# A four-stage transformer block: first distances before the second turn, squares and subtractions on GpSimd, lane loads from ScalarE's queue, preparation loads behind them

## The reference

```python
x = x + tanh(g_xattn[0]) * dtw_align(ctx, layernorm(x))     # stage 1
x = x + tanh(g_ffn[0])   * moe_64_experts_top8(layernorm(x), ...)   # stage 2
x = x + tanh(g_xattn[1]) * attention(layernorm(x), ctx, ctx, Wq..bo)  # stage 3
x = x + tanh(g_ffn[1])   * moe_8_experts_top2(layernorm(x), ...)    # stage 4
```

```python
D = sqrt(max(aa + bb - 2 * ctx @ xn.T, 0))          # 77 x 512 distances, per batch
R[i, j] = D[i, j] + min(R[i-1, j], R[i, j-1], R[i-1, j-1])
path = backtrack(R) from (76, 511) to (0, 0)
aligned[j] = sum of ctx[i] over the path's cells (i, j)
```

## Time and profile before

| what | value |
|---|---|
| median of 3 runs | 759.21 us (757.62 to 759.25) |
| the profiled execution's own time | 759.99 us |
| its span, first to last instruction | 758.3 us |
| PE / DVE / ACT / POOL busy | 656.2 / 570.3 / 397.4 / 349.5 us |
| mean granted TensorE clock | 0.903 |

### The profile page before, as it was taken

How to read it: one execution, slowest core, us unless ns; L and a number is a source line. 1 busy time by engine, 2 the same in 40 slices (tenths; PEclk the granted TensorE clock), 3 DMA queues, 4 the chain that set the end, 5 groups by cost and what they waited for, 6 DMA issues and landing times.

```text
span 758.3 us, 13278 instructions
## 1 busy us (share of the span) xinstructions
PE 656.2 (87%) x3528; PEld 502.7 (66%) x3528; DVE 570.3 (75%) x1608; ACT 397.4 (52%) x707; POOL 349.5 (46%) x326
## 2 busy tenths in 40 slices
PE   5329523889999999999999779988989999999997
PEld 2116313667888888888888546655768888888885
DVE  6579895857777777777777784889867777777775
ACT  4624220555655655565556544544456555655654
POOL 4000130565666666666666560000356666666664
PEclk9855555699999999999999968998799999999999
DMA  6565543067776776677677100000166656665761
GB/s 155 76 86 169 166 131 62 7 147 151 161 145 139 159 154 141 146 157 154 135 154 158 28 2 2 2 2 13 38 122 153 151 133 160 156 144 138 159 153 56
DMA packets 85148, 86.50 MB, mean 114 GB/s; under 512 B 41109, under 2 KB 65294, under 8 KB 82166
## 3 DMA queue, kind: packets, MB, share of 16 engines
q1 hardware_dynamic: 77340, 79.80, 49.4%
q10 hardware_dynamic: 7769, 6.25, 3.1%
HBM read 76.84 MB, written 9.17 MB: 113 GB/s over the span
## 4 chain that ended last, share of the span: by engine, by line
PE 71%; DVE 12%; DMA 5%; issue 4%; SPq 4%; ACT 2%; POOL 2%; ACTq 1%; DVEq 0%; POOLq 0%
PE bank L1203 7%; PE bank L1204 7%; PE bank_quad L1359 7%; PE bank L1205 7%; PE bank_pair L1203 7%; PE bank_quad L1356 7%; PE bank_pair L1204 7%; PE bank_pair L1205 7%; PE bank_quad L1357 7%; DMA scr_d<-arena 3%; PE bank_pair L1252 2%; PE bank L1295 2%; DVE arena L1670 1%; PE bank_pair L1175 1%; DVE rden L1799 1%
## 5 line engine op out<-in xcount | busy, mean ns | idle before, releaser
L803 POOL TENSOR_TENSOR act_lo<-arena,act_hi 128x512 fp32r<-128x512 f32 x232 | 300.3, 1294 | 191.2 <-ACT act_hi L1003 147.7
L1017 ACT ACTIVATE arena<-bank 128x512 f32<-128x512 f32 x232 | 138.8, 598 | 183.3 <-PE bank L1205 183.3
L1903 DVE TENSOR_TENSOR bank_pair<-arena,bank_pair 128x512 f32<-128x512 f32 x220 | 152.4, 693 | 99.9 <-ACT arena L1017 70.6
L1911 DVE TENSOR_TENSOR arena<-bank_pair,arena 128x512 f32<-128x512 f32 x220 | 152.1, 691 | 17.8 <-DMA arena<-scr_mask 5.7
L1003 ACT ACTIVATE act_hi<-arena 128x512 fp32r<-128x512 f32 x232 | 144.5, 623 | 14.4 <-DVE arena L1901 7.5
L1359 PE MATMUL bank_quad<-act_lo,w_hi 128*128 128x512 f32 x232 | 93.0, 401 | 4.0 <-POOL act_lo L803 4.0
L1203 PE MATMUL bank_pair<-xn_hi,w_hi 128*128 128x512 f32 x232 | 92.8, 400 | 3.5 <-DVE arena L1911 1.8
L1203 PE MATMUL bank<-xn_hi,w_hi 128*128 128x512 f32 x232 | 93.1, 401 | 0.0
L1204 PE MATMUL bank<-xn_hi,w_lo 128*128 128x512 f32 x232 | 93.1, 401 | 0.0
L1356 PE MATMUL bank_quad<-act_hi,w_hi 128*128 128x512 f32 x232 | 93.0, 401 | 0.0
L1204 PE MATMUL bank_pair<-xn_hi,w_lo 128*128 128x512 f32 x232 | 92.1, 397 | 0.0
(11 more groups left out here) (252 smaller groups left out, 981.1 us busy)
## 6 DMA issues: line engine op xcount, KB each, us to landing
arena<-scr_mask SPq DMA_DIRECT2D x94, 512.0 KB, 6.6
scr_w<-prep_out ACTq DMA_DIRECT2D x25, 192.0 KB, 2.4
w_raw<-scr_w SPq DMA_DIRECT2D x25, 192.0 KB, 6.3
w_raw<-in_L_ffn_expert_gate_k SPq DMA_DIRECT2D x32, 64.0 KB, 5.9
w_raw<-in_L_ffn_expert_up_k SPq DMA_DIRECT2D x32, 64.0 KB, 5.6
w_raw<-in_L_ffn_expert_down_k SPq DMA_DIRECT2D x64, 32.0 KB, 5.3
prep_in<-in_L_ffn_wg SPq DMA_DIRECT2D x21, 64.0 KB, 2.0
prep_in<-in_L_ffn_wu SPq DMA_DIRECT2D x21, 64.0 KB, 2.4
```

Of the source, the lines that this page charges most:

```text
L803: nc.gpsimd.tensor_tensor(act_lo[:, k % 2, :], act_a[:, k % 2, :], act_hi[:, k % 2, :].bitcast(F32), ALU.subtract).then_inc(FF[f]["alo"], 1)
L1017: nc.scalar.activation(act_s[:, k % 2, :], ps[4 + k % 2][:], ACT.Silu).then_inc(FF[f]["silu"], 1)
L1903: nc.vector.tensor_tensor(ps[6 + i][:], act_s[:, i, :], ps[6 + i][:], ALU.mult).then_inc(FF[f]["t"], 1)
L1911: nc.vector.tensor_tensor(act_a[:, i, :], ps[6 + i][:], mask[:, j, 512 * k:512 * (k + 1)], ALU.mult).then_inc(FF[f]["act"], 1)
```

## The change

It does the following.

1. The order of the front: ACT takes the first square root before it writes the zeros, which it writes in two parts (`blank`); PE does `distances(0)` before `turn(0, 1)`, then the tables; ACT's order is written out in `norm0`.
2. POOL makes the squares of batches 2 and 3 (`square`) and the subtraction of batches 0 to 2 (`POOL_SUBS`), in place of ACT and DVE.
3. `x` of batches 2 and 3 is loaded only when the keys have landed. `ctx_sb` is cleared in two parts.
4. ACT's queue loads the attention weights, all first lanes but one, and stores one of the first rows; SP's queue has all later rows and lanes.
5. SP loads 3 groups of the preparation ahead of the rows, in place of 4, and issues the first expert weights, the routers, the output bias and the ones only behind group 5.
6. PE's meeting sums stand behind groups 8 to 10 in place of 7 to 10; ACT's `split_first(0)` stands ahead of group 7.

```diff
-    PATH_AT, PREP = 22, 4
-    MEET_PARTS, VALUE_AT = {7: range(0, 4), 8: range(4, 8), 9: range(8, 12), 10: range(12, CH)}, 16
+    PATH_AT, PREP, PREP_FIRST, RAW_AT, SPLIT_GROUP = 22, 4, 3, 5, 7
+    BLANK, POOL_SUBS, POOL_SQUARES = 30, 3, 2
+    MEET_PARTS, VALUE_AT = {8: range(0, 5), 9: range(5, 9), 10: range(9, CH)}, 16
...
+        def first_lanes(engine, d, b):
+            engine.wait_ge(s_dst[b], 32)
+            load_lanes(engine, d, b, 0, FIRST_ROWS, s_dld)
+
+        def later_rows(engine):
+            for d in range(2):
+                for b in range(B):
+                    store_dist(engine, d, b, FIRST_ROWS, DIST_ROWS, s_dst2)
+
+        def later_lanes(engine):
             for b in range(B):
                 engine.wait_ge(s_dst[b], 32)
...
+            for d in range(2):
+                engine.wait_ge(s_dst2, 16 * 2 * B)
+                for b in range(B):
+                    load_lanes(engine, d, b, FIRST_ROWS, SLOTS, s_dld2)
...
             for b in range(B):
+                if b == 2:
+                    sp.wait_ge(s_ctx, 16 * len(CTX_PARTS))
                 sp.dma_start(x_res[:, TPB * b:TPB * (b + 1), :], x_t[b]).then_inc(s_x[b], 16)
...
-            raw0(1, 1)
-            for g in range(PREP):
+            for g in range(PREP_FIRST):
                 load_prep(sp, g, *prep_span(g))
-            sp.wait_ge(s_zero, 16 * -(-LSLOT // SLOTS))
+            sp.wait_ge(s_zero, 16 * -(-LSLOT // BLANK))
             for b in range(B):
                 sp.wait_ge(s_dist, b + 1)
-                for d in range(2):
+                for d in range(2 if b + 1 < B else 1):
                     store_dist(sp, d, b, 0, FIRST_ROWS, s_dst[b])
-                if b >= 1:
-                    sp.wait_ge(s_dst[b - 1], 32)
-                    for d in range(2):
-                        load_lanes(sp, d, b - 1, 0, FIRST_ROWS, s_dld)
-            sp.wait_ge(s_dst[B - 1], 32)
-            for d in range(2):
-                load_lanes(sp, d, B - 1, 0, FIRST_ROWS, s_dld)
-            later_rows(sp, 0)
-            later_lanes(sp, 0)
-            for g in range(PREP, GROUPS[1]):
+            sp.wait_ge(s_blank, 2)
+            first_lanes(sp, 0, B - 1)
+            later_rows(sp)
+            later_lanes(sp)
+            for g in range(PREP_FIRST, GROUPS[1]):
                 load_prep(sp, g, *prep_span(g))
+                if g == RAW_AT:
+                    shared0()
+                    raw0(1, 1)
+                    sp.dma_start(router[0][:], r0_w).then_inc(s_rw[0], 16)
+                    sp.dma_start(bo_all[:], bo.partition_broadcast(P)).then_inc(s_gbo, 16)
+                    sp.dma_start(router1_rows[:], r1_w).then_inc(s_rw[1], 16)
+                    sp.dma_start(scr_one.rearrange("(p c) -> p c", c=P), ones[0:TOK // P, :]).then_inc(s_one, 16)
...
+            for b in range(B):
+                normalise(0, b)
+                if b - 1 >= B - POOL_SQUARES:
+                    square(b - 1)
+            square(B - 1)
+            for b in range(POOL_SUBS):
+                pool.wait_ge(s_root, b + 1)
+                nc.gpsimd.tensor_tensor(d2[0:KROWS, b, 0:S], d2[0:KROWS, b, 0:S], droot2[0:KROWS, b, :], ALU.subtract).then_inc(s_fpool, 1)
...
+            def norm0():
+                root(0, 0)
+                blank(0, BLANK)
+                context()
+                root(0, 1)
+                high(0, 0)
+                for m, w in enumerate((Wq, Wk, Wv, Wo)):
+                    act.dma_start(w4[:, m, :], w).then_inc(s_aw, 16)
+                root(0, 2)
+                blank(BLANK, SLOTS)
+                lane_tables()
+                high(0, 1)
+                root(0, 3)
+                high(0, 2)
+                act.wait_ge(s_lc, 1)
+                dist_root(0)
+                high(0, 3)
+                for b in range(1, B):
+                    dist_root(b)
...
+            for d in range(2):
+                first_lanes(act, d, 0)
...
+            act.wait_ge(s_dist, B)
+            store_dist(act, 1, B - 1, 0, FIRST_ROWS, s_dst[B - 1])
+            for d in range(2):
+                first_lanes(act, d, 2)
+            act.wait_ge(s_gate, 32)
+            nc.scalar.activation(tgate[:], gates[:], ACT.Tanh).then_inc(s_tg, 1)
+            first_lanes(act, 1, B - 1)
             nc.scalar.activation(ctxT4[:], ctxT[:].unsqueeze(2).broadcast_to([P, B, RHEADS, KEYS]), ACT.Copy).then_inc(s_c4, 1)
-            later_rows(act, 1)
...
-            norm(0, distances)
+            turn(0, 0)
+            distances(0)
+            tables()
+            turn(0, 1)
+            turn(0, 2)
+            distances(1)
+            turn(0, 3)
+            distances(2)
+            distances(3)
...
-                inv = done(nc.vector.tensor_tensor(d2[rows, b, 0:S], d2[rows, b, 0:S], droot2[rows, b, :], ALU.subtract))
+                if b < POOL_SUBS:
+                    dve.wait_ge(s_fpool, POOL_SQUARES + b + 1)
+                else:
+                    inv = done(nc.vector.tensor_tensor(d2[rows, b, 0:S], d2[rows, b, 0:S], droot2[rows, b, :], ALU.subtract))
```

More of the change, by code:

```diff
@@ L392, in program @@
         s_dst = [sem(f"dist_stored{b}") for b in range(B)]
-        s_dst2 = [sem(f"dist_later_stored{d}") for d in range(2)]
+        s_dst2 = sem("dist_later_stored")
         s_dld = sem("dist_lanes")
@@ L544, in _ @@
             sp.dma_start(gates[:, 2:4], g_ffn.partition_broadcast(P)).then_inc(s_gate, 16)
-            sp.dma_start(router[0][:], r0_w).then_inc(s_rw[0], 16)
-            for m, w in enumerate((Wq, Wk, Wv, Wo)):
-                sp.dma_start(w4[:, m, :], w).then_inc(s_aw, 16)
+            sp.wait_ge(s_blank, 1)
+            for first in range(0, LSLOT, BLANK):
+                n = min(BLANK, LSLOT - first)
+                sp.dma_start(scr_d[:, :, first:first + n].rearrange("b c s w -> (b c) (s w)"),
+                             dl[0:B * CH, 0:n].rearrange("p s w -> p (s w)")).then_inc(s_zero, 16)
             for m, v in enumerate((bq, bk)):
@@ L550, in _, with shared0 @@
             sp.dma_start(bv_row[:], bv.rearrange("(o p) -> o p", o=1)).then_inc(s_aw, 16)
[L551 to L564, removed]
+            def shared0():
+                sp.wait_ge(s_pool, 2)
+                sp.dma_start(w_raw[:, 0, 0:I0], sg0).then_inc(FF_RAW[0][0], 16)
+                sp.dma_start(w_raw[:, 0, UP:UP + I0], su0).then_inc(FF_RAW[0][0], 16)
+                for k in range(2):
+                    sp.dma_start(w_raw[k * I0 // 2:(k + 1) * I0 // 2, 0, DOWN:DOWN + P],
+                                 sd0[k * I0 // 2:(k + 1) * I0 // 2]).then_inc(FF_RAW[0][0], 16)
             def raw0(g, j):
@@ L877, in query, with blank @@
                                      bias=bias2[:, 0:1]).then_inc(s_qhi, 1)
+            def blank(first, last):
+                nc.scalar.activation(dl[:, first:last], ones[:, 0:CW].unsqueeze(1).broadcast_to([P, last - first, CW]),
+                                     ACT.Copy, scale=0.0).then_inc(s_blank, 1)
+            def norm0():
[17 more added lines that the diff above has]
+                    dist_root(b)
             def norm(k):
@@ L881, in norm @@
                     root(k, b)
-                    if k == 0 and b == 0:
-                        context()
-                    if b >= 1 and not (k == 0 and b == B - 1):
+                    if b >= 1:
                         high(k, b - 1)
-                    if k == 0 and b == 1:
-                        lane_tables()
                     if k == 2 and b >= 2:
                         query(b - 2)
-                if k == 0:
-                    act.wait_ge(s_lc, 1)
-                    dist_root(0)
-                    high(0, B - 2)
-                    dist_root(1)
-                if k in (0, 2):
+                if k == 2:
                     high(k, B - 1)
-                if k == 2:
                     query(B - 2)
                     query(B - 1)
-            act.wait_ge(s_cz, 1)
-            for first, keys in CTX_PARTS:
+            for n, (first, keys) in enumerate(CTX_PARTS):
+                if n == 2:
+                    act.wait_ge(s_cz, 2)
                 act.dma_start(ctx_sb[first:first + keys.stop - keys.start], ctx_1024[:, keys].rearrange("b k d -> k b d")).then_inc(s_ctx, 16)
@@ L905, in _ @@
             nc.scalar.activation(root_one[:], ones[:, 0:1], ACT.Sqrt)
-            nc.scalar.activation(dl, ones[:, 0:CW].unsqueeze(1).broadcast_to([P, SLOTS, CW]), ACT.Copy, scale=0.0).then_inc(s_blank, 1)
-            norm(0)
-            for b in range(2, B):
-                dist_root(b)
-            act.wait_ge(s_gate, 32)
-            nc.scalar.activation(tgate[:], gates[:], ACT.Tanh).then_inc(s_tg, 1)
-            act.wait_ge(s_aw, 16 * 8)
+            norm0()
+            act.wait_ge(s_blank, 2)
+            for d in range(2):
+                first_lanes(act, d, 0)
+            act.wait_ge(s_aw, 16 * 7)
             nc.scalar.activation(wq_hi[:], w4[:, 0, :], ACT.Copy)
@@ L946, in value_block @@
```

(8 more changed lines are left out.)

40 lines of the change are left out of this document (19 added, 21 removed).

## The result

The changed kernel takes 763.22 us (median of 9 runs, 761.26 to 765.93), the kernel before 759.17 us (median of 9 runs beside them). The ratio is 1.0044, with a 95% interval of 1.0028 to 1.0059: about 3.3 us by the ratio, while the two medians stand 4.05 us apart. The profiled execution took 762.78 us with a span of 761.1 us, against 759.99 and 758.3 for before.

What follows compares the result with a forecast made beforehand. It took the distance stores, then PE's groups waiting for SP's loads, to bound the meeting: 78.8 us against 77.4, +1.4. Added to the profiled 759.99 that makes 761.4, less 0.8 to the median 760.6; range 757.0 to 763.4.

Steps and rivals of the forecast that it cites:

- What bounds the kernel: First stage: distance stores, then DVE's wave and PE's groups bound the meeting-column search; all later work moves with it unchanged.
- Rival A: The forecast itself: PE's late groups set the meeting, DVE's idle before the search grows to 4 us; 760.6 us, chance 0.50.
- first store: SP's issue of the first distance store, at the end of the front: from 24.36 to 24.0 us.
- T: Moment SP may load the last batch's lanes, all first rows being in DRAM: 37.6 us, 1.5 us earlier.
- batch 0's distances: DVE's sum for batch 0, which releases SP's store: ready at 24.0 us, bounds 22.9 to 25.0.
- over 1.3 us of overlap that adds 0.6: DVE's product and sum beside POOL's next subtraction: 1.4 us alone, 0.6 us more from the overlap.
- rival B: Slower: same chain but T isn't won, +3.6 us, 762.8; with PE's slow pace throughout, +4.4; chance 0.33.
- The drain: First-row stores run at a rate per write, not a latency per store: 13.6 us after the first, bounds 13.0 to 14.8.
- From T on: SP's later rows 9.5 us, lane loads 3.3, groups 4.9, moved transfers 6.0, then PE's groups and sums to 78.8 us.
- Rival C: Faster: the wave sets the meeting, PE's groups coming 3.4 us sooner; 755.5 us with T at 36.0; chance 0.17.
- Does nothing: Stores' drain is a latency per store, T follows batch 3's distances to some 36, meeting at 77.2; inside Rival A's share.
- By it the two square moves cost nothing: By the skill's rule that GpSimd and VectorE share SBUF interfaces, POOL's squares cost nothing and its subtractions do.

Runs made afterwards that it cites:

- e5: The changed kernel timed once more with no edit; ratio 1.0067 to the kernel before.
- e6: The changed kernel with the twelve moved transfers behind group 10 and all subtractions back on DVE; ratio 0.9955 to the kernel before.
- e1: The changed kernel with the twelve moved transfers behind group 10 in place of 5, split_first ahead of group 11; ratio 0.9975 to the kernel before.
- e2: The changed kernel with all subtractions back on DVE, squares still on POOL; ratio 1.0018 to the kernel before.
- e3: The changed kernel with ACT's four attention weight loads behind the last root of the distances; ratio 1.0058 to the kernel before.
- e4: The changed kernel with the last batch's second first-rows store issued by SP in place of ACT; ratio 1.0066 to the kernel before.
- e9: The same kernel as e6, run again; ratio 0.9935 to the kernel before.
- e10: e6 with the squares of batches 2 and 3 back on ACT; ratio 0.9940 to the kernel before.
- e11: e6 with ACT's four attention weight loads behind the last root; ratio 0.9955 to the kernel before.
- e7: The kernel before with eleven front transfers (expert weights, routers, ones) behind group 10, split_first ahead of group 11; ratio 0.9983 to the kernel before.

## Why the prediction was right and wrong

**What bounds the kernel: right.** The stage moved with the meeting, and all behind it by the same distance (679.9 against 680.9 us, at the bound of the 1 us that I allowed; e5 with 682.6 and e6 with 685.0 show that one pair of executions can't hold this to 1 us).

**Rival A's mechanism, the forecast's own: right, and shown by e1.** The moved transfers stand ahead of group 6, PE waits for its load, all 15 sums stand behind it, DVE waits for the last. With them behind group 10 the wait is gone and the ratio falls from 1.0044 (1.0067 in e5) to 0.9975.

**Its size: off, 3.8 us on the search where the sum had 1.4.** Term by term, for the profiled execution:

| term | forecast | measured |
|---|---|---|
| last normalised tile | 18.15 | 18.24 |
| POOL's first subtraction ends | 22.0 | 24.1 |
| DVE's product and sum | 2.0 | 3.2 |
| first store | 24.0 | 27.4 |
| batch 3's distances | 29.6 | 33.4 |
| first store to T | 13.6 | 12.0 |
| T | 37.6 | 39.4 |
| T to group 3's first load | 13.2 | 13.0 |
| groups 3 to 5 on SP | 4.9 | 5.1 |
| moved transfers to group 6's first | 6.0 | 6.5 |
| group 6's first issue to the landing of its third | 3.15 | 3.3 |
| group 6 on PE to the search | 13.95 | 13.8 |

The mis-sized term is T, 1.8 us late, and its failing step is batch 0's distances at "24.0 us". It failed twice. I took PE to be at its faster pace "then" (15.2 us). For `turn(0, 1)` that was right (0.63 us for its four turns, to 14.6 us), but I let the pace hold for `distances(1)` too, with batch 3's copy at 19.2 us. PE paused for 1.41 us ahead of `turn(0, 2)`, and the first passes of `distances(1)` took 1.12 and 1.06 us; the copy was there at 21.7 us and the subtraction ended 2.1 us late, 1.6 of it by the pace, as e5 shows. And "over 1.3 us of overlap that adds 0.6" took the stretch from 554 to 970 ns as a slowdown by a factor. It is a stop. DVE's product begins beside POOL's second subtraction, which ends at 22.77 + 2.50 = 25.27 us, and ends 0.55 us later, at 25.82. The sum begins beside the third, which ends at 26.77, and ends at 27.32, again 0.55 later. In e2 the sum ends 0.55 us after the square beside which it began (22.66 and 23.21). Of its 0.69 us DVE has 0.14 done when POOL is through. What I gave as rival B's case ("batch 0 comes at 27 us: +4.4") is what this execution shows. That its price is near the 3.8 us measured is in part luck: the first store came at 27.4 us, and the time from there to T was 1.6 us shorter than I took it to be.

**The drain: near in size, not shown as a rule.** From the first store to T the changed order gave 12.0, 13.8 (e5), 14.0 (e1), 13.8 (e2), 14.3 (e3), 13.0 (e4), 13.8 (e6), 15.5 (e9), 14.0 (e10) and 14.8 us (e11), around the 13.6 that I took. e4 speaks against a fixed time behind the last store: 6.6 us from its issue to T, where the changed kernel had 3.8. But in the changed kernel, e3, e4 and e5 the first store moves between 25.3 and 27.4 us and T stays within 0.2 us of 39.5, while e1, the same program up to there, has its first store at 27.2 and T at 41.2. So the failed steps above explain the first store and not the whole of T. e2, e6 and e10, where the first store is at 22.4 to 23.3 us, have T at 36.3 to 37.1. From batch 3's distances to T it took 6.0 us in the changed kernel, 7.8 (e5), 7.9 (e1), 6.4 (e2), 8.3 (e3), 7.0 (e4), 6.7 (e6), 6.1 (e9), 6.5 (e10) and 7.7 (e11), a narrower spread than that behind the first store. So "T follows the first store's issue plus the drain" is no better borne out than a rule from batch 3. Which part is tied to which store, and what the stores wait for while the DMA engines move nothing, these runs leave open.

**From T on: 0.6 us short, in other executions more.** Here 0.5 of it are the moved transfers. The later rows' drain was put at 9.5 us, between 9.2 and 9.9. From their first issue to SP's next lane loads it took 9.1 (48.93 - 39.81) in the changed kernel, but 10.2 (50.20 - 39.96) in e5, 10.5 (48.01 - 37.49) in e2 and 10.2 (47.38 - 37.15) in e6. In e5 this puts group 6 on PE at 68.60 us, 29.0 after T, and the search 1.2 us later than in the first execution. The bounds of the term were too narrow.

**Rival C: its mechanism was real, but not in this kernel.** "The wave sets the meeting" is what e1, e6, e9, e10 and e11 show. The 3.4 us by which PE's groups would have had to come sooner are there as soon as the moved transfers go behind group 10. My sum for its time was wrong, though. I had the wave end at 74.5 us in one place and at 75.0 in another; with before's 34.0 us of slots from T + 2.55 it ends at 74.2 for T at 37.6. So e6's search, 3.8 us earlier, matches the "3.7 earlier" for T at 36.0 us by luck: it had T at 36.8.

**"Does nothing": it didn't happen, and its sum didn't follow.** With batch 3's distances only 0.4 us earlier, a T that follows them would be at 38.7 and not at some 36. A T that follows them exactly is refuted: they came at 33.4 us in the changed kernel and at 31.8 in e5, with T at 39.4 and 39.6. The same pair refutes a fixed time behind the first store.

**The chances.** B had 0.33, and against it stood "only that PE ought to speed up". In e5 PE did, and the kernel was as slow: DVE's stop (3.2 us for product and sum, in place of 2.0) and the drains at 13.8 and 10.2 us (in place of 13.6 and 9.5) took the place of PE's pace. So B's result had several roads to it, and I had counted two.

**"By it the two square moves cost nothing": true here only by the order.** DVE had no two-input operation while POOL squared. In e2 a square beside DVE's sum stretched the sum to 1.58 us.

**Not settled.** The 0.25% of e1 is not what its one profile shows: the search was 0.6 us later than in before. In that execution T was 1.8 us later than in the changed kernel, which is the same program up to there. With T at 39.5 the search would be at 76.4; this is argued, not shown.

## What to carry to other kernels

When a batch of transfers is moved in a queue, look at what is issued behind its new place, and who has other work queued behind those: here six microseconds of issuing, which cost little at the front (taking most of them away gained 0.17% in e7) and left PE without a gap behind group 10, stood ahead of a load in front of which the last sums of the critical path waited. A long wait on the engine that uses a result (DVE ahead of the search) and a queue that never rests (SP) are the sign. Work offloaded to a second engine must be costed with its place in that engine's order, and as time in which the first can't run where both have two inputs.

## What the runs showed of the hardware

**Two-input operations of DVE and POOL hold each other up, almost one behind the other.** DVE's 104x512 product or sum takes 0.69 us alone; beside POOL's two-input operations 1.74, 1.47 (changed and e5), 1.58 (e2) and 1.41 us (e6). Each of them ends 0.55 us after the POOL instruction beside which it began. It goes both ways: e6's second square, which began 0.50 us before the end of a DVE subtraction, took 1.40 us in place of 1.04. In e9 this overlap was 0.31 us and the square took 1.21, in e11 0.61 and 1.51. In all these cases the later instruction was longer by the overlap less 0.14 us. One doesn't show it: POOL's third subtraction began 0.24 us before the end of DVE's product and took 1.19 us, and the first, with DVE idle, 1.24. In e6 first DVE, then POOL:

```profile
20.77 1.41 DVE L1623 TENSOR_TENSOR arena<-arena 104x512 f32<-104x512 f32 x1
```

```profile
20.23 1.40 POOL L774 TENSOR_TENSOR arena<-arena 128x512 f32<-128x512 f32 x1 [1.04 <-ACT arena L872]
```

The Trainium skill (SBUF — State Buffer, "Who interferes with whom") calls the shared port pair an exclusive lock; the rows agree but for the 0.14 us and the third subtraction.

**The same program, two paces on PE.** Of the ten profiles of the new order, `distances(1)` began with passes of 0.93 to 1.12 us in five (changed, e1, e2, e4, e9) and of 0.61 to 0.64 us in the other five. The granted clock from 16.4 to 19.7 us was 0.50, 1.00, 0.50, 1.00 and 0.64 in the first five and 1.00 in the others, so a 1.00 in this column doesn't prove the faster pace. Before's slow passes from 13.56 to 17.16 us stood at 1.00 too.

**Issues on ACT's queue got long.** The four weight loads took 0.36, 1.28, 1.30 and 1.23 us, 4.2 together, where I had assumed 1.9:

```profile
9.90 1.28 ACTq L910 DMA_DIRECT2D w<-in_L_xattn_Wk  x1
...
13.81 0.21 ACT L866 ACTIVATE std<-veps 128x4 f32<-128x4 f32 x1 [3.23 <-issue]
```

SP's issues of the same stretch were stretched too (1.28 us at 11.19 us). The third root stood behind them for 3.23 us. e3 removed the wait and e11 did so in the faster order, and neither gained.
